# Three shared expert blocks by token halves, with expert buffers and loads in another order

## The reference, cut to what matters

```python
x = x + xattn(layernorm(x), ctx_768, ...)
x = x + attn(layernorm(x), ...)          # 16 heads, causal
x2 = layernorm(x).reshape(-1, D)         # 512 tokens
topk_idx, topk_w = router(x2, gate_w, bias_e)     # sigmoid, 2 of 4 groups, then 4 of 16 experts
routed = sum over e of combine[:, e] * (relu2(x2 @ up_w[e].T) @ down_w[e].T)    # inner width 256
shared = relu2(x2 @ shared_up.T) @ shared_down.T                                # inner width 1024
x = x + routed + shared
```

## Time and profile before

| what | value |
|---|---|
| three runs | 387.63, 389.01, 391.02 us; median 389.01 |
| profiled execution | 390.19 us, of which 388.1 us are the span from first to last instruction |
| mean granted clock of PE | 0.956 of full |
| busy in the span | PE 87%, PEld 61%, DVE 63%, ACT 49%, POOL 21% |
| bytes moved | 69.70 MB, 180 GB/s over the span |

### The profile page before, as it was taken

The page is one execution under the profiler, slowest core; times in us unless marked ns, Lnnn a source line. Parts: engine busy times, 40 slices in busy tenths (PEclk is TensorE's granted clock), DMA queues, the critical chain, the costliest instruction groups (busy, mean ns, idle before and its releaser), DMA issues.

```text
span 388.1 us, 6900 instructions
## 1 busy us (share of the span) xinstructions
PE 337.9 (87%) x2492; PEld 235.7 (61%) x2492; DVE 243.1 (63%) x484; ACT 189.3 (49%) x425; POOL 82.9 (21%) x103
## 2 busy tenths in 40 slices
PE   1998879999999999988777899996299999999794
PEld 1976657677677667667566779884144444444252
DVE  3755867646588296475666759933025767787577
ACT  2547365525565665534656714500034777776600
POOL 5400000000012012212233140044034444442000
PEclk9999899999999999988968999999599999999998
DMA  7893599856233352290000460489934334322493
GB/s 199 310 413 105 176 394 417 315 217 222 81 94 102 132 208 93 69 392 0 30 0 30 146 262 0 122 315 397 426 122 138 110 115 130 113 84 83 120 382 123
DMA packets 16225, 69.70 MB, mean 180 GB/s; under 512 B 2880, under 2 KB 3392, under 8 KB 13632
## 3 DMA queue, kind: packets, MB, share of 16 engines
q1 hardware_dynamic: 12672, 57.72, 40.1%
q0 software_dynamic: 3520, 11.54, 8.6%
HBM read 61.91 MB, written 7.34 MB: 178 GB/s over the span
## 4 chain that ended last, share of the span: by engine, by line
PE 70%; DVE 14%; ACT 6%; issue 6%; POOL 2%; DMA 1%; SPq 0%; DVEq 0%; ACTq 0%
PE bank L1711 10%; PE bank L1324 10%; PE bank L1679 10%; PE bank L1326 9%; PE bank L1325 9%; PE bank L1550 7%; DVE res L1304 3%; PE bank L1648 2%; ACT hw L787 2%; PE bank L1449 2%; PE bank L1690 2%; PE bank L1520 1%; PE bank L1475 1%; PE bank L1459 1%; DVE cT L1100 1%
## 5 line engine op out<-in xcount | busy, mean ns | idle before, releaser
L1679 PE MATMUL bank<-WX,xsT 128*32 128x256 f32 (+1 forms) x256 | 39.7, 412 | 11.6 <-issue 9.9
L1550 PE MATMUL bank<-ring,wT 128*128 128x384 f32 x128 | 43.9, 486 | 0.0
L1711 PE MATMUL bank<-WX,hsT 128*32 128x512 f32 (+1 forms) x128 | 38.1, 598 | 2.9 <-ACT ys_h L832 1.8
L1679 PEld LDWEIGHTS bank<-WX,xsT 128*32 128x32 f32 x256 | 18.5, 117 | 33.7 <-issue 21.5
L1100 DVE TENSOR_TENSOR cT<-ring_T,cT 128x512 fp32r<-128x512 f32 x48 | 30.5, 684 | 5.8 <-ACT cT L670 5.8
L1265 DVE COPY down_copy<-WX 128x1024 f32 x32 | 21.2, 700 | 17.6 <-PE bank L1711 17.6
L1550 PEld LDWEIGHTS bank<-ring,wT 128*128 128x128 f32 x128 | 23.7, 190 | 13.4
L1243 DVE COPY xsT<-bank 128x512 f32<-128x512 f32 x20 | 13.7, 684 | 28.2 <-PE bank L1648 28.2
L670 ACT CAST cT<-ring_T 128x512 fp32r<-128x512 f32 x48 | 26.8, 618 | 8.3 <-PE bank L1326 8.1
L570 POOL TENSOR_TENSOR rstd<-var,mhalf 128x1 f32<-128x1 f32 x12 | 7.4, 613 | 109.9 <-DVE var L901 109.9
L1711 PE MATMUL bank<-down_copy,hsT 128*32 128x512 f32 x192 | 30.7, 598 | 0.0
(11 more groups left out here) (298 smaller groups left out, 865.9 us busy)
## 6 DMA issues: line engine op xcount, KB each, us to landing
WX<-in_experts SPq DMA_DIRECT2D x16, 1024.0 KB, 6.4
ring_T<-in_ctxT SPq DMA_DIRECT2D x16, 768.0 KB, 7.3
ring<-in_ctx SPq DMA_DIRECT2D x16, 768.0 KB, 4.5
yr<-y_rows SPq DMA_DIRECT2D x8, 512.0 KB, 8.1
raw<-in_experts SPq DMA_DIRECT2D x3, 1024.0 KB, 5.0
res<-in_x SPq DMA_DIRECT2D x4, 256.0 KB, 4.5
raw<-in_wqT SPq DMA_DIRECT2D x4, 256.0 KB, 5.1
raw<-in_woT SPq DMA_DIRECT2D x1, 1024.0 KB, 12.1
```

Source lines behind the costliest of these rows:

```text
L1550: last = mm(bank[B_O][:, 0:TD], wT[:, g % 2, k * P:(k + 1) * P], ring[:, g % RING, k, :], start=(c == 0 and k == 0), stop=(c == NCH - 1 an ...
L1679: last = mm(bank[B_H[g % 2]][q * SLOT:(q + 1) * SLOT, 0:IC * P], xsT[:, g % 2, c * P + q * SLOT:c * P + (q + 1) * SLOT], w, start=c == 0, ...
L1711: last = mm(bank[B_Y[g % 2]][q * SLOT:(q + 1) * SLOT, :], hsT[:, g % 2, m * P + q * SLOT:m * P + (q + 1) * SLOT], w, start=m == 0, stop=m ...
```

## The change

Block 2 joins blocks 0 and 1 in going by halves of the tokens (HB = 3 blocks). The first halves' steps are new, weights are split from step 21 on, and the shared weights, `gh`, `gl` and the routing's tables move to other places, so that the expert loads wait for other things. After the loop PE's order is new: ups of three second halves with `counts` in the third, block 3's ups, down half 0, `entries`, down half 1, down half 2 with `group_rows_T(0)` between its two tiles, `group_rows_T(1)`; then `group_rows_T` and DVE's `group_rows` run one group further ahead than before. The diff, cut to its core:

```diff
+        HB = NSH - 1
+        u_w = [at(f"u_w{e}", [P, 2, HALF], wx_place((6, 12, 3, 4)[e]), F32R) for e in range(NSH)]
+        d_w = [at(f"d_w{e}", [P, 2, HALF], wx_place((8, 15, 14)[e]), F32R) for e in range(HB)]
-        gh = at("gh", [P, 2, IC, T], wx_place(4), F32R)
+        gh = at("gh", [P, 2, IC, T], wx_place(9), F32R)
         gl = at("gl", [P, 2, IC, T], wx_place(5), F32R)
-        gh2 = at("gh2", [P, 2, IC, T], hw_at, F32R)
-        gl2 = at("gl2", [P, 2, IC, T], qk_s_at, F32R)
+        gh2, gl2 = (at(n, [P, IC, T], wx_place(13) + i * HALF * 2 * 2, F32R) for i, n in enumerate(("gh2", "gl2")))
...
-        UP_SPLIT, DOWN_SPLIT = (25, 26), (28, 30)
-        UP_STEP = ((26, 27), (28, 28))
-        DOWN_STEP = ((30, 31), (31, 32))
+        UP_SPLIT, DOWN_SPLIT = (21, 25, 27), (22, 24, 28)
+        UP_STEP = ((25, 26), (26, 27), (28, 29))
+        SQUARE_STEP, GATED_STEP = (27, 28, 31), (28, 29, 32)
+        DOWN_STEP = ((29, 30), (31, 31), (33, 33))
...
-            return B_UP[e][0] if h else B_POST
+            return ((B_O, B_POST, B_POST), (B_POST, 6, 0))[h][e]
...
-            for e in (0, 1, 2, 9):
+            for e in (0, 1, 2):
                 load_routed(e)
             for e in range(FIRST):
                 sp.wait_ge(u_lo, e + 1)
...
             load_routed(10)
             load_routed(11)
-            sp.wait_ge(up_mm, IC * FIRST + IC)
-            load_routed(3)
+            for e, place in enumerate((6, 12, 3)):
+                sp.wait_ge(up_mm, HB + e + 1)
+                load_routed(place)
             sp.wait_ge(up_mm, IC * NSH)
+            load_routed(4)
+            sp.wait_ge(acc_mm, 1)
             load_routed(8)
             sp.wait_ge(idx_ok, 1)
-            for e in (7, 12, 13):
+            load_routed(7)
+            sp.wait_ge(acc_mm, 2)
+            for e in (5, 9, 15):
                 load_routed(e)
-            sp.wait_ge(acc_mm, FIRST)
-            load_routed(4)
-            load_routed(5)
-            sp.wait_ge(acc_mm, FIRST + 1)
-            for e in (6, 14, 15):
-                load_routed(e)
+            sp.wait_ge(acc_mm, HB)
+            load_routed(13)
+            load_routed(14)
...
             def down_hi(e):
+                act_e.wait_ge(raw_in[e % 2], (e // 2 + IN_SLOT[e % 2] + 1) * 16)
+                if e == 0:
+                    act_e.wait_ge(att_mm, NB)
+                elif e == 1:
+                    act_e.wait_ge(wo_mm, NB // 2)
...
-                        for e in range(FIRST, NSH):
-                            up_hi(e)
-                            if e < NSH - 1:
-                                down_hi(e)
+                        up_hi(NSH - 1)
...
-                for e in range(FIRST):
-                    if step == UP_STEP[e][1] + 1:
+                for e in range(HB):
+                    if step == SQUARE_STEP[e]:
                         squares_half(e, 0)
...
-                    if b == NB - 1:
-                        up_lo(FIRST)
-                        down_lo(FIRST)
...
-                for e in range(FIRST):
-                    if step == UP_STEP[e][1] + 2:
+                for e in range(HB):
+                    if step == GATED_STEP[e]:
                         gated_half(e, 0)
...
             weights()
             rows_of_groups()
             gated_half(1, 1)
-            gated(FIRST)
+            gated_half(2, 1)
...
             group_rows(0)
+            group_rows(1)
             dve.wait_ge(acc_mm, NSH - 1)
...
-                if g + 1 < NG:
-                    group_rows(g + 1)
+                if g + 2 < NG:
+                    group_rows(g + 2)
...
+            def first_ups(step, late=False):
+                for e in range(HB):
+                    for m in range(IC):
+                        if step == UP_STEP[e][m] and late == (e > 0):
+                            pe.wait_ge(xlo_ok, norm_no["last", 1] + 1)
+                            if e == 0:
+                                pe.wait_ge(o_ok, NB)
+                            elif e == 1:
+                                pe.wait_ge(qkv_ok, 3 * NB - 1)
+                            else:
+                                pe.wait_ge(relu_ok, e)
+                            up_half(e, 0, m)
+            def first_downs(step):
+                for e in range(HB):
+                    for b in range(2):
+                        if step == DOWN_STEP[e][b]:
+                            pe.wait_ge(d_lo, e + 1)
+                            pe.wait_ge(g_ok, e + 1)
+                            if e == 0:
+                                pe.wait_ge(rexp_ok, 2)
+                            down_tile(e, b, first=e == 0, final=e == HB - 1)
...
             for step in range(1, STEPS):
+                first_ups(step)
                 if (u := unit_at(step, 0)) is not None and u % 2 == 0:
                     pair_scores(u)
...
-                if step <= U_STEP + UNITS + 1:
-                    first_experts(step)
-
+                first_ups(step, late=True)
                 if (u := unit_at(step, 2)) is not None and u % ROWS == ROWS - 1:
...
                     last.then_inc(a_mm, 1)
+                first_downs(step)
                 if (b := batch_at(step, POST)) is not None:
...
-            pe.wait_ge(relu_ok, FIRST + 1)
-            up(2, counts)
-            pe.wait_ge(relu_ok, FIRST + 2)
-            up(3)
+            pe.wait_ge(relu_ok, HB)
+            for e in range(HB):
+                for m in range(IC):
+                    up_half(e, 1, m)
+                    if e == HB - 1 and m == 0:
+                        counts()
+            pe.wait_ge(relu_ok, HB + 2)
+            up(NSH - 1)
+            pe.wait_ge(rexp_ok, NB)
             pe.wait_ge(cnt_ok, 1)
+            down_half(0)
             entries()
-            down_half(0)
             down_half(1)
-            down(2, final=True)
...
-            group_rows_T(0)
+            down_half(2, lambda: group_rows_T(0))
+            group_rows_T(1)
             for g in range(NG + 2):
...
-                if g + 1 < NG:
-                    group_rows_T(g + 1)
+                if g + 2 < NG:
+                    group_rows_T(g + 2)
```

More of the change, by code:

```diff
@@ L807, in _ @@
                     nc.scalar.activation(r_exp[:, b, :], bank[rows_bank(b)][:, 0:NE], ACT.Exp, scale=-1.0).then_inc(rexp_ok, 1)
-            for e in range(FIRST):
+            for e in range(HB):
                 squares_half(e, 1)
-            for e in range(FIRST, NSH):
-                squares(e)
+            squares(NSH - 1)
             def group_hidden(g):
@@ L934, in inverse_sums @@
                 V_.reciprocal(hrd[:, b, r * HT:(r + 1) * HT], hden[:, b, r * HT:(r + 1) * HT]).then_inc(hrd_ok, 1)
-            def gated(e):
-                for m in range(IC):
-                    dve.wait_ge(sq_ok, IC * e + m + 1)
-                    V_.tensor_tensor(inner(gl, gl2, e, m), act[:, e % 2, m, :], f32(inner(gh, gh2, e, m)), ALU.subtract).then_inc(g_ok, 1)
             def gated_half(e, h):
-                dve.wait_ge(sq_ok, FIRST * h + e + 1)
-                V_.tensor_tensor(gl[:, e, :, half(h)], act[:, e, :, half(h)], f32(gh[:, e, :, half(h)]), ALU.subtract).then_inc(g_ok, 1)
+                dve.wait_ge(sq_ok, HB * h + e + 1)
+                V_.tensor_tensor(inner(gl, gl2, e)[:, :, half(h)], act[:, e % 2, :, half(h)], f32(inner(gh, gh2, e)[:, :, half(h)]),
+                                 ALU.subtract).then_inc(g_ok, 1)
             def flat(t):
@@ L1380, in query_constants, with up @@
                 last.then_inc(c_mm, 1)
-            def up(e, between=None):
+            def up(e):
                 pe.wait_ge(u_lo, min(e + 1, NSH - 1))
@@ L1390, in up @@
                                         (xT_h[:, c, :], xT_l[:, c, :]), c == 0, c == DC - 1)
-                        if between is not None and m == 0 and c == 1:
-                            between()
                     last.then_inc(up_mm, 1)
@@ L1397, in down_tile @@
                     o = m * D
-                    last = split_mm(bank[B_ACC[b]][:], (inner(gh, gh2, e, m)[:, tok(b)], inner(gl, gl2, e, m)[:, tok(b)]),
+                    last = split_mm(bank[B_ACC[b]][:], (inner(gh, gh2, e)[:, m, tok(b)], inner(gl, gl2, e)[:, m, tok(b)]),
                                     (d_part(e, 0)[:, o:o + D], d_part(e, 1)[:, o:o + D]), first and m == 0, final and m == IC - 1)
                 return last
-            def down(e, final=False):
-                pe.wait_ge(d_lo, e + 1)
-                pe.wait_ge(g_ok, IC * (e + 1))
-                for b in range(NB):
-                    last = down_tile(e, b, final=final)
-                last.then_inc(acc_mm, 1)
             def up_half(e, h, m):
@@ L1418, in up_half @@
                     last.then_inc(up_mm, 1)
-            def first_experts(step):
-                for e in range(FIRST):
+            def first_ups(step, late=False):
+                for e in range(HB):
                     for m in range(IC):
```

(19 more changed lines are left out.)

56 lines of the change are left out of this document (25 added, 31 removed).

## The result

The changed kernel takes 393.71 us (median of 4 runs, 392.32 to 394.70), the kernel before, run beside it, 388.92. The ratio is 1.0115, 95% interval 1.0061 to 1.0170: 2.4 to 6.6 us slower, where I had forecast 4 us faster and a range to 391. A repeat in the first experiment gave 392.05 us (10 runs) against 389.05, ratio 1.0073 (1.0036 to 1.0109). So the loss is 3 to 5 us, 0.7 to 1.2%.

What follows compares the result with a forecast made beforehand. PE, 87% busy, bounds the kernel, with a 9.9 us wait for late expert loads. Despite the loop's end at +3.0 us (3.4 - 0.4), group 4's ups gain 5.4; clock costs 1.4: 389.01 - 4.0 = 385.0 us, range 380 to 391.

Steps and rivals of the forecast that it cites:

- the term for the loop's end: Step 33: block 2's two down tiles, waiting for its gated half, delay the last logits by 3.4 us.
- the bounds: Limits of the loop's-end delay: +1.2 us with the low part there in time, +6.2 us with the 12 products at half rate.
- The self-attention: Six up halves in the loop: last batch's output projection starts 0.4 us earlier; range -2 to +5 us.
- rival 1: Loop ends no later: the low clock at 188.8 to 197.0 vanishes and pays for step 33; 382.0 us, chance 0.20.
- The row numbers: Behind the loop: PE's work up to `entries` stays 18.8 us, so row numbers come at 257.9 us.
- Loads: Six instead of eight expert loads issued behind the row numbers; group 1's wait of 9.9 us is gone.
- PE's two idle stretches: Waits of some 4 to 5 us each, for the gathers of group 0 and group 4.
- Gather 4: Rows for group 4 arrive at 280.8 us; 281.2 by the same distance from the row numbers, 280 by bytes.
- From there to group 4's ups: Transposes, down 0, up 3, down 1 take 6.6 us behind gather 4, plus 1.4 us for the lowered clock.
- Later groups at nothing: From group 4 on, transposes one group further ahead cost nothing; 3 us over 16 groups kept for the range.
- Rivals 1 and 2: The second: loop ends 3 to 4 us later, gather waits and pauses cost clock; about 388.4 us, chance 0.20.
- Rival 3: Up halves at half clock on the loop's path; last logits more than 7 us later, past 237; 393 us, chance 0.10.

Runs made afterwards that it cites:

- the first experiment: Run 1: the changed kernel once more, with no edit; 392.05 us (10 runs).
- run 2: Changed kernel with POOL's subtraction for block 3 made to wait for block 2's gated half; 389.08 us (10 runs).
- run 3: Changed kernel with block 2's first-half squares moved from step 31 to 29, its gated half from 32 to 30; 386.03 us (4 runs), 385.40 in a repeat.
- run 4: Changed kernel with the two down tiles of step 33 behind the last logits instead of ahead; 392.50 us (10 runs).
- Run 7: Kernel of run 3 with the three writes of zero rows issued behind gather 5 instead of ahead of gather 4; 385.09 us (4 runs).
- Run 8: Kernel of run 3 with each group's down products ahead of the transposes of rows two groups on; 389.18 us (10 runs).
- runs 9 and 10: 9: kernel of run 3, three zero-row writes behind gather 11, 388.71 us. 10: also block 2's last down tile ahead of group 0's transposes, 388.21 us.

## Why the prediction was wrong

**The step that failed** is the term for the loop's end: "so the tiles start at about 230.6 and take 12 x 0.233 = 2.8 us ... +3.4 us". Its mechanism was right; tiles and gated half stood where I said, in the order I said. Its size was off in two ways.

- The 0.69 us for the gated half was taken from `rows_lo`, as the same shape. But `rows_lo` reads one operand from PSUM (`bank`) and one from SBUF (`xT_h`), the gated half both from SBUF. Here POOL's subtraction ran beside it, and it took 2.83: 2.1 us. Moving that one instruction of POOL's returned 3.0 us of the end time (run 2). The trace of before already had that subtraction in this very place, begun while `rows_lo` (229.25, 0.69 us) still ran:

```profile
229.76 2.38 POOL L605 TENSOR_TENSOR uw<-raw,uw 128x1024 fp32r<-128x1024 f32 x1
```

  It ended at 232.14. With the 0.55 us that the other pair of rows shows behind POOL's end, the gated half is done near 232.7 and not at 230.6, an estimate from rows of before alone: the 2.1 us could have been read there.
- The tiles ran at 1.2 GHz, 5.25 us in place of 2.8, so 2.5 us more. I had that in my upper bound of +6.2, and wrote the reason for it ("since PE pauses just ahead of them"), but took the value without it. Both together exceeded the bound: the term measured 8.1 us.

With the low part ready earlier, both are gone at once and the term is the lower bound, +1.2 (run 3). The choice between the bounds was the prediction: at +1.2 the change wins 3 to 4 us, at +3.4 plus collision and clock it loses 3 to 5.

**The self-attention** (-0.4 us) came out at -0.5 in the one pair of traces it was made for: 58.8 us from the last o tile's end to the last output projection, where before had 59.3. More profiles say otherwise. The three executions profiled with the old order took 59.3, 58.1 and 56.5 us, mean 58.0; the eleven with the six up halves in the loop 58.8 to 61.5, mean 60.0. The scatter is 2 to 3 us, and the two groups overlap. Counted from the span's start they don't: the last output projection begins at 219.93 to 221.62 in the three and at 222.67 to 224.07 in the eleven, 2.6 us apart in the mean, 0.6 of it there at the end of the o tiles. So this term too was most likely too small, by 2 us or more; that the up halves are the reason isn't shown, since a kernel with them alone wasn't tried. With +2 for it the sum is 8.1 + 2.0 - 7.2 = +2.9, an estimate, beside +3.0 by the medians in the repeat and +4.8 in the first result. The clock did rise in the stretch I had named (1.00 in place of 0.80 from 188.80 to 197.00, PE busy 7.17 us of it), without moving the end of the stage forward. That fits what the prediction held against rival 1, that the chain through ACT and DVE sets it.

**The row numbers.** 18.76 us of work behind the loop were to stay 18.8. It is 259.41 - 240.62 = 18.8. Right; and run 4 shows that it is PE's chain that sets this distance.

**Loads.** The 9.9 us wait is gone, group 1's ups start at 276.57 with no wait for a load. Right.

**PE's two idle stretches**, of 4 to 5 us each by the prediction, came as three waits of 1.0, 1.8 and 3.3 us. PE asked for group 0's rows 9.4 us behind the start of `entries` (268.85) and not 7.7, since the granted clock was 0.82 there and part of down half 1 went 0.43 us a product. In the repeat they were two, of 4.2 and 3.9 us.

**Gather 4.** I put it at 280.8 with the row numbers at 257.9, so 22.9 us behind them (22.1 by bytes, 23.3 by the distance of before). It came 22.6 behind (row numbers at 263.92, transposes at 286.53), in the repeat 24.0. Right in the first trace, a little early by the second. Run 7 shows what held it: with the zeros out of the way it came at most 17.4 us behind them (257.75 and 275.15). It stood behind the zeros in its own queue. The prediction said so, but weighed only what taking loads from the other queue would do. The rule of the Trainium skill named there ("DMA: Bandwidth & Descriptors", "Queues, rings and completion order"), turns between queues, agrees with this: the loads stayed in their queue, and the gather still gained 6.4 us once its own queue was clear.

**From there to group 4's ups**: 6.6 + 1.4 for the clock. It took 294.93 - 286.53 = 8.4. Down 0 alone lost 1.7 at half clock (3.62 against 1.92). Right within half a microsecond.

**Later groups at nothing**: 4.39 us each before and after, right for the order as changed. Run 8 shows how thin it was: with downs and transposes swapped, the same work takes 0.28 us more a group.

**The rivals.** Rivals 1 and 2 had the loop end at +0 and at +3 to 4 us; it was +9.3. Rival 3's time, 393, and its sign for "wrong", last logits past 237, both came true, but not by its mechanism: the up halves in the self-attention didn't fall to half clock (granted clock 0.95 on average from 190 to 223 us). The tiles of step 33 did, together with a collision that stood in no case of mine. I gave 0.10 to that side, and the time lay beyond the upper end of the range.

## What to carry to other kernels

When a change puts a DVE result on the critical path, look at what POOL does in those same microseconds, not only at DVE's queue. If both read two operands from SBUF, add POOL's whole remaining time. A wait of PE ahead of products can cost the wait and then the slower clock behind it: 4.24 and 2.09 us ahead of the tiles did (runs 1 and 2), 2.31 and 2.82 us ahead of group 3's ups did not (runs 9 and 10, 1.93 us for the 32 products). Put the second price into the range of a new wait, or place the producer two steps earlier, which here was worth 6 to 7 us. And a helper write that is off the path, such as rows of zeros, belongs neither ahead of a gather that is due nor three in a row ahead of a scatter; one at a time, behind scatters, it cost nothing here (61.41 us for fourteen groups against 61.42).

## What the runs showed of the hardware that I had not expected

- DVE's two-operand subtraction of 128x512 took 0.68 us alone, 1.53 us beside the end of a POOL product and 2.83 us beside a whole POOL subtraction of 128x1024 (2.36 us). It ended 0.55 to 0.56 us behind POOL's end both times.
- It goes the other way too. In the trace of after a small POOL product of 128x1 started just behind one of DVE's weight subtractions; the first fence is DVE, the second POOL at that place and at another, with DVE not in its way:

```profile
207.17 1.22 DVE L893 TENSOR_TENSOR u_w<-raw,u_w 128x1024 fp32r<-128x1024 f32 x1
```
```profile
207.33 1.47 POOL L572 TENSOR_TENSOR rstd<-var,mhalf 128x1 f32<-128x1 f32 x1 [1.71 <-DVE var L903]
...
227.81 0.56 POOL L572 TENSOR_TENSOR rstd<-var,mhalf 128x1 f32<-128x1 f32 x1 [11.26 <-DVE var L903]
```

  DVE's ended at 208.39, POOL's at 208.80. A layernorm waited for that value.
- With the DMA engines 89% busy (run 9, from 258.00 us to the start of group 3's ups), two loads issued 6.7 us sooner moved the products that wait for them by 0.1 us (runs 9 and 10).
- Three indirect writes in a row on POOL's queue (4.0 us of issue) were followed by one group of 9.13 and 9.18 us in place of 4.39 in two kernels, and by none when spread. In run 9 PE, ACT and DVE all stood or went slowly until 307.6; the profile calls the releaser "remote", and which transfer it was stays open.
